# Cross-attention scores on two float32r parts, two heads stacked in 64-row tiles

## What is computed

```
q = heads(x @ Wq)              # 32 heads of 16
k, v = split(ctx @ Wkv)        # heads likewise
q, k = rope(q, pos), rope(k, pos)
p = softmax(q @ k.T / sqrt(16))
out = (p @ v) @ Wout + bout    # then x = layernorm(x + out)
```

## Time and profile before

| | us |
|---|---|
| median of 3 runs | 3319.63 |
| lowest, highest | 3304.61, 3321.81 |
| profiled execution | 3316.54 |
| its span | 3314.8 |
| cross attention in it | about 2415 to 3120 |

### The profile page before, as it was taken

One profiled execution on the slowest core, in us unless ns is written; L12 is line 12 of the kernel. 1 busy time (PEld: TensorE's weight loads), 2 busy tenths in 40 slices (PEclk: granted clock), 3 DMA queues, 4 the chain that ended last, 5 costly groups with the idle time before them and its releaser, 6 DMA issues.

```text
span 3314.8 us, 50665 instructions
## 1 busy us (share of the span) xinstructions
PE 2716.1 (82%) x20138; PEld 1454.0 (44%) x20154; DVE 1958.6 (59%) x3064; ACT 1433.1 (43%) x2577; POOL 1177.7 (36%) x1118
## 2 busy tenths in 40 slices
PE   5788888876677676589988898888768989899787
PEld 3565656553223232268845444444433333333244
DVE  3323232333689889956526566656655657476477
ACT  3232333320545555423426262635315546465555
POOL 0443333441566666600023625243243424241000
PEclk8888888887888888799998999998879989899999
DMA  2222222130330304032332424243155435252301
GB/s 87 71 59 62 52 78 60 47 87 14 121 116 13 127 26 140 13 140 95 137 108 86 128 90 125 93 122 130 39 117 107 105 69 112 61 109 53 118 26 39
DMA packets 209370, 280.04 MB, mean 84 GB/s; under 512 B 84640, under 2 KB 111680, under 8 KB 208240
## 3 DMA queue, kind: packets, MB, share of 16 engines
q1 hardware_dynamic: 209136, 276.81, 29.4%
HBM read 192.08 MB, written 59.12 MB: 76 GB/s over the span
## 4 chain that ended last, share of the span: by engine, by line
PE 39%; DVE 10%; issue 5%; ACT 4%; POOL 2%; DMA 1%; SPq 0%; ACTq 0%; DVEq 0%; POOLq 0%
PE ps L236 7%; PE ps L3368 4%; PE ps L1846 4%; PE ps L1857 4%; PE ps L3355 4%; PE ps L3341 3%; PE ps L3300 3%; PE ps L3332 2%; PE ps L2512 1%; ACT arena L3446 1%; PE ps L2520 1%; DVE arena L2775 1%; DVE arena L1434 1%; DMA arena<-arena 1%; DVE arena L2773 1%
## 5 line engine op out<-in xcount | busy, mean ns | idle before, releaser
L236 PE MATMUL ps<-arena 128*128 128x512 f32 (+3 forms) x1280 | 473.6, 522 | 18.3 <-ACT arena L2612 6.1
L3545 DVE TENSOR_REDUCE arena<-ps 128x1 f32<-128x512 f32 x512 | 330.3, 685 | 229.2 <-PE ps L3341 227.8
L3446 ACT ACTIVATE arena<-ps 128x512 f32<-128x512 f32 x512 | 287.8, 597 | 283.2 <-PE ps L3355 279.7
L1466 POOL TENSOR_TENSOR arena<-arena 128x1024 f32<-128x1024 f32 x128 | 311.0, 2430 | 192.9 <-DVE arena L1458 192.9
L1482 PE MATMUL ps<-arena 128*128 128x512 f32 x512 | 267.2, 662 | 55.8 <-POOL arena L1466 55.5
L1458 DVE TENSOR_TENSOR_SCAN arena<-ps,arena 128x1024 f32<-128x1024 f32 x128 | 291.5, 2278 | 32.9 <-ACT ps L1449 32.9
L236 PEld LDWEIGHTS ps<-arena 128*128 128x128 f32 (+2 forms) x1296 | 193.2, 154 | 252.3 <-issue 172.9
L1449 ACT ACTIVATE ps<-arena 128x511 f32<-128x511 f32 x256 | 165.1, 679 | 188.3 <-DVE arena L1458 188.1
L576 POOL TENSOR_TENSOR arena<-arena 128x31 f32<-128x31 f32 (+15 forms) x217 | 130.1, 600 | 324.2 <-DMA arena<-d_a 307.8
L3355 PE MATMUL ps<-arena 99*128 99x512 bf16 x512 | 198.4, 390 | 45.3 <-ACT arena L3446 33.4
L3341 PE MATMUL ps<-arena 96*128 96x512 bf16 x512 | 201.4, 395 | 19.1 <-issue 15.4
(11 more groups left out here) (352 smaller groups left out, 5254.1 us busy)
## 6 DMA issues: line engine op xcount, KB each, us to landing
arena<-d_bc SPq DMA_DIRECT2D x32, 1024.0 KB, 5.7
arena<-d_x SPq DMA_DIRECT2D x24, 1024.0 KB, 6.8
arena<-d_parts SPq DMA_DIRECT2D x192, 128.0 KB, 4.6
d_x<-arena SPq DMA_DIRECT2D x64, 256.0 KB, 2.5
arena<-arena SPq DMA_DIRECT2D x128, 128.0 KB, 2.1
arena<-in_D_wlm SPq DMA_DIRECT2D x12, 1024.0 KB, 6.6
d_parts<-arena SPq DMA_DIRECT2D x32, 384.0 KB, 2.4
d_signs<-arena SPq DMA_DIRECT2D x32, 256.0 KB, 2.1
```

The lines of the kernel that those rows point to most:

```text
L236: ins = pe.e.matmul(ps[:m, :n], lhsT(k), rhs(k), start=(k == 0), stop=(k == chunks - 1))
L1466: pool.e.tensor_tensor(h, h, s.bc[:, turn % s.SLOTS, 1], ALU.mult).then_inc(*pool.up("scan_hC"))
L3446: act.e.activation(s.E[:, k % 2, j], s.rexp.bank((u, i)), ACT.Exp).then_inc(*s.rexp.empty(act, (u, i)))
L3545: dve.e.tensor_reduce(s.mx[:, u % 2, t, h:h + 1], s.rmax.bank((u, m)), AX.X, ALU.max, negate=True).then_inc(*s.rmax.empty(dve, (u, m)))
```

## The change

The scores are made on two float32r parts in place of three bfloat16 parts: high x high, high x low and low x high, 3 x 16 = 48 rows, and two rows more for the maximum. Even heads lie on partitions 0 to 49, odd heads on partitions 64 to 113, so each score matmul takes one 64-row half of the array (tile size 64 x 128, tile position row 0 or row 64), and the two of a pair write different PSUM banks. The PE program issues two exp scores and then two max scores, and the odd pieces of both steps come after that. The maximum scores of two heads alternate, and so do the reduces. rope() has two operations where it had four behind the rotation. The stacked loads are again six DMAs of 128 KB per unit and side, in runs of 2 KB where they were 1 KB; what is written to DRAM before them is 512 KB in place of 384 KB. The ones come by two DMAs at the start of the stage (sp_one_rows), and the memsets for them go. The stage's buffers become tensors of their own at fixed places (PLACED), and two of them go.

```diff
-    Q_PARTS = (0, 1, 0, 2, 1, 0)
-    K_PARTS = (0, 0, 1, 0, 1, 2)
-    N = 6 * 16
+    Q_PARTS = (0, 0, 1)
+    K_PARTS = (0, 1, 0)
+    N = 3 * 16
...
-        s.Qs, s.Ks = carve(s.SLOTS, s.HU, L, dt=BF16), carve(s.SLOTS, s.HU, L, dt=BF16)
+        s.Qs, s.Ks = carve(s.SLOTS, s.HU // 2, L, dt=F32R), carve(s.SLOTS, s.HU // 2, L, dt=F32R)
...
-        for a in range(3):
-            sp.e.dma_start(s.Qs[96 + a:97 + a, u % s.SLOTS, s.G * half:s.G * (half + 1)],
-                           s.mT[s.G * a:s.G * (a + 1), half, :]).then_inc(*sp.up(f"cross_max_rows{half}", 16))
+        for p in range(2):
+            at = 64 * p + s.N
+            sp.e.dma_start(s.Qs[at:at + 2, u % s.SLOTS, 2 * half:2 * half + 2].bitcast(F32),
+                           s.mT[4 * p:4 * p + 4, half, :].bitcast(F32)).then_inc(*sp.up(f"cross_max_rows{half}", 16))
...
-            sp.e.dma_start(dst[16 * a:16 * a + 16], d[:, :, part, :].rearrange("h d l -> d h l")).then_inc(*sp.up(f"cross_stack_{'qk'[w]}", 16))
+            for p in range(2):
+                at = 64 * p + 16 * a
+                sp.e.dma_start(dst[at:at + 16].bitcast(F32), d[p::2, :, part, :].rearrange("h d l -> d h l")).then_inc(*sp.up(f"cross_stack_{'qk'[w]}", 16))
+
+    def sp_one_rows(self, sp):
+
+        s = self
+        sp.e.wait_ge(*sp.at_all("cross_ones"))
+        for p in range(2):
+            at = 64 * p + s.N
+            sp.e.dma_start(s.Ks[at:at + 2].rearrange("p a h l -> p (a h) l").bitcast(F32), spread(s.one[:2], 1, s.SLOTS * s.HU // 2)).then_inc(*sp.up("cross_one_rows", 16))
...
-        hi, mid, lo = (s.parts[:, w, a] for a in range(3))
+        hi, lo = (s.parts[:, w, a] for a in range(2))
         e.tensor_copy(hi, s.m1[:, w]).then_inc(*eng.up_step("cross"))
         eng.e.wait_ge(*eng.at_step("cross"))
-        e.tensor_tensor(s.rest[:, w], s.m1[:, w], hi, ALU.subtract).then_inc(*eng.up_step("cross"))
-        eng.e.wait_ge(*eng.at_step("cross"))
-        e.tensor_copy(mid, s.rest[:, w]).then_inc(*eng.up_step("cross"))
-        eng.e.wait_ge(*eng.at_step("cross"))
-        e.tensor_tensor(lo, s.rest[:, w], mid, ALU.subtract).then_inc(*eng.up(f"cross_parts_{n}"))
+        e.tensor_tensor(lo, s.m1[:, w], hi.bitcast(F32), ALU.subtract).then_inc(*eng.up(f"cross_parts_{n}"))
...
-        s, slot, h, t = self, u % self.SLOTS, m // T, m % T
+        s, slot = self, u % self.SLOTS
+        hh, t, p = m // (2 * T), m // 2 % T, m % 2
...
-        pe.e.matmul(s.rmax.bank((u, m)), s.Qs[:s.N, slot, h, t * P:(t + 1) * P], s.Ks[:s.N, slot, h, :],
+        rows = slice(64 * p, 64 * p + s.N)
+        pe.e.matmul(s.rmax.bank((u, m)), s.Qs[rows, slot, hh, t * P:(t + 1) * P], s.Ks[rows, slot, hh, :],
...
-        pe.e.matmul(s.rexp.bank((u, i)), s.Ks[:s.N + 3, slot, s.G * g + j, k * P:(k + 1) * P], s.Qs[:s.N + 3, slot, s.G * g + j, :],
+        hh, p = 2 * g + j // 2, j % 2
+        rows = slice(64 * p, 64 * p + s.N + 2)
+        pe.e.matmul(s.rexp.bank((u, i)), s.Ks[rows, slot, hh, k * P:(k + 1) * P], s.Qs[rows, slot, hh, :],
...
-            for m in range(s.STEPS):
+            for m in range(1, s.STEPS, 2):
                 if s.unit(i) is not None:
+                    s.pe_exp(pe, i, m - 1)
                     s.pe_exp(pe, i, m)
                 if s.unit(i + 1) is not None:
+                    s.pe_max(pe, i + 1, m - 1)
                     s.pe_max(pe, i + 1, m)
                 if m % s.G == 1:
...
-                if m in misc:
-                    s.pe_misc(pe, misc[m])
+                for at in (m - 1, m):
+                    if at in misc:
+                        s.pe_misc(pe, misc[at])
...
-        e.tensor_copy(s.identb, s.ident).then_inc(*dve.up("cross_identb"))
-        for a in range(2):
-            e.memset(s.ones[:, a], s.ONES).then_inc(*dve.up("cross_ones"))
         s.rope(dve, 0, 1)
-        for a in range(2, s.SLOTS):
-            e.memset(s.ones[:, a], s.ONES).then_inc(*dve.up("cross_ones"))
...
-                    h, t = m // T, m % T
+                    h, t = m // (2 * T) * 2 + m % 2, m // 2 % T
```

More of the change, by code:

```diff
@@ L3029 @@
     VW = 32
[L3030 to L3031 removed]
+    ONCE = ("cross_weights", "cross_late", "cross_ones", "cross_one_rows", "cross_half_pi")
     EARLY = ("cross_weights", "cross_x", "cross_pos", "cross_ctx")
@@ L3048, in __init__ @@
         s.rows_from = carve.at
-        s.Qs, s.Ks = carve(s.SLOTS, s.HU, L, dt=BF16), carve(s.SLOTS, s.HU, L, dt=BF16)
+        s.Qs, s.Ks = carve(s.SLOTS, s.HU // 2, L, dt=F32R), carve(s.SLOTS, s.HU // 2, L, dt=F32R)
         s.rows_to = carve.at
-        s.ones = carve.t[96:99, carve.at - s.SLOTS * s.HU * L // 2:carve.at].rearrange("p (a n) -> p a n", a=s.SLOTS)
-        s.wo, s.identb, s.half_pi, s.xT = carve(C, D), carve(P, dt=BF16), carve(1), carve(C, L)
+        s.one = carve(L)
+        s.wo, s.half_pi, s.xT = carve(C, D), carve(1), carve(C, L)
         s.cos, s.sin = carve(2, L), carve(2, L)
-        s.raw, s.m1, s.m2, s.rest = carve(2, L), carve(2, L), carve(2, L), carve(2, L)
-        s.parts = carve(2, 3, L, dt=BF16)
-        s.mx, s.mr = carve(2, T, s.HU), carve(T, s.G)
-        s.mp = carve(2, T, 3, s.G, dt=BF16)
-        s.mT = carve(2, L, dt=BF16)
+        s.raw, s.m1, s.m2 = carve(2, L), carve(2, L), carve(2, L)
+        s.parts = carve(2, 2, L, dt=F32R)
+        s.mx = carve(2, T, s.HU)
+        s.mp = carve(2, T, 2, 2, 2, dt=F32R)
+        s.mT = carve(2, L, dt=F32R)
         s.rs = carve(T, s.G)
@@ L3310, in pe_misc @@
             pe.e.wait_ge(*R.at_free(pe, name))
-            if u == half == 0:
-                pe.e.wait_ge(*pe.at_all("cross_identb"))
             for t in range(T):
-                ins = e.transpose(ps.bitcast(BF16)[:3 * s.G, t * P:(t + 1) * P], s.mp[:, half, t].rearrange("p a h -> p (a h)"), s.identb)
+                ins = e.transpose(ps[:2 * s.G, t * P:(t + 1) * P], s.mp[:, half, t].rearrange("q p a h -> q (p a h)").bitcast(F32), s.ident)
         elif what == "turn":
@@ L3351, in pe_exp @@
             pe.e.wait_ge(*pe.at_all("cross_ones"))
+            pe.e.wait_ge(*pe.at_all("cross_one_rows"))
         if k == j == 0:
@@ L3426, in act_misc @@
                 act.e.wait_ge(*act.on(f"cross_max_rows{name[2]}", u - 1))
-            ins = e.activation(s.mT[:3 * s.G, name[2]], ps.bitcast(BF16)[:3 * s.G, :L], ACT.Copy)
+            ins = e.activation(s.mT[:2 * s.G, name[2]], ps[:2 * s.G, :], ACT.Copy)
         else:
@@ L3480, in dve_before @@
         s, e = self, dve.e
+        e.memset(s.one[:2], 1.0).then_inc(*dve.up("cross_ones"))
         e.memset(s.V[:, :, :, :, 16:17], 1.0).then_inc(*dve.up("cross_ones"))
@@ L3524, in dve_parts @@
             dve.e.wait_ge(*s.ring.at_filled(dve, ("mT", u - 1, half)))
-        mx = s.mx[:, u % 2, :, s.G * half:s.G * (half + 1)]
+        mx = s.mx[:, u % 2, :, s.G * half:s.G * (half + 1)].rearrange("q t (h p) -> q t p h", p=2)
         dve.e.wait_ge(*s.rmax.at_emptied(dve, (u, (half + 1) * s.STEPS // 2 - 1)))
-        mp = s.mp[:, half]
-        e.tensor_copy(mp[:, :, 0, :], mx).then_inc(*dve.up_step(st))
+        hi, lo = s.mp[:, half, :, :, 0, :], s.mp[:, half, :, :, 1, :]
+        e.tensor_copy(hi, mx).then_inc(*dve.up_step(st))
         dve.e.wait_ge(*dve.at_step(st))
-        e.tensor_tensor(s.mr, mx, mp[:, :, 0, :], ALU.subtract).then_inc(*dve.up_step(st))
-        dve.e.wait_ge(*dve.at_step(st))
-        e.tensor_copy(mp[:, :, 1, :], s.mr).then_inc(*dve.up_step(st))
-        dve.e.wait_ge(*dve.at_step(st))
-        e.tensor_tensor(mp[:, :, 2, :], s.mr, mp[:, :, 1, :], ALU.subtract).then_inc(*dve.up(f"cross_max_parts{half}"))
+        e.tensor_tensor(lo, mx, hi.bitcast(F32), ALU.subtract).then_inc(*dve.up(f"cross_max_parts{half}"))
     def dve_all(self, dve):
```

11 lines of the change are left out of this document (5 added, 6 removed).

## The result

The changed kernel takes 3347.34 us (median of 4 runs, 3344.05 to 3357.28), the kernel before 3319.64 us (3304.61 to 3321.81). The ratio is 1.0098, with a 95% interval of 1.0062 to 1.0135 (the two medians alone give 1.0083): slower by about 1%. Forecast were 3306 us and a range from 3282 to 3345. The time lies outside the range, and on the other side of no change.

What follows compares the result with a forecast made beforehand. The prediction took a loop of values matmul, exp score, exponentials and freed bank as the bound. Units +5, batch ends −17, front −1 and last unit +1 sum to −12 us; forecast 3306 us, range 3282 to 3345.

Steps and rivals of the forecast that it cites:

- What bounds the kernel: Plain units: a loop of values matmul, exp score, two exponentials and a freed bank, 3.11 us, sets the pace.
- The price of a score: Score matmuls on PE: a pair in 0.22 us, 0.11 each; a first score after another shape pays +0.11.
- rival 1: Score pairs: halves run one after the other, 0.22 apart; about 3355 us, break-even at 0.14 between partners; chance 0.12.
- the tail term: Loop-bound intervals, fourth exp score to values matmul: 0.11 + 0.11 + 0.31 = 0.53 us against 0.54, nothing gained.
- The PE-bound intervals: Plain unit: steps 13 to 17 from 4.63 to 4.43 us (−0.2); steps 5 to 9 and 9 to 13 together −0.15.
- The change of tile shape: PE, between matmuls of different tile shape: costs 0.09 us, 0.31 where 0.22 is usual.
- the dearer case: Change of tile shape drains TensorE: 0.16 us each, five times 0.07 more a unit, about 5 us in all.
- Batch ends: Iterations 4 and 8: new order covers 4.9 of 5.64 us of waits and shortens the long y by 3.1; −8 each.
- The third boundary: Batch end at iteration 12, where the y pieces stand without xT: −1 us.
- Front: Start of the stage: rope's two operations fewer save 2.1 us once, loads stay as they were; net −1.
- The clock: Plain units: clock expected to stay at 1.00; a fall got chance 0.07, argued against from the exp-only stretch.
- rival 2: Plain units: clock falls as work per score shrinks and gaps remain; +42 us, 3348 us; chance 0.07.

Runs made afterwards that it cites:

- the second pair of profiles: The changed kernel and the kernel before, each run once more unchanged; the two profiles differ by 30.6 us.
- the filler: Changed kernel with unread whole-array matmuls added ahead of mT, turn and aT from iteration 13 on; 3371.55 us in one run.
- other banks: Changed kernel with three PSUM banks for exp scores and two for max scores, in place of two and three; 3323.59 us, ratio 1.0033.

## Why the prediction was wrong

**What bounds the kernel: right.** The loop of bank, score, exponential and values matmul sets the plain unit. Two scores now go at once, and the units grew all the same.

**The price of a score: wrong, and the step with the largest share in the units.** I took 0.11 from score to score. The partner costs 0.003, so the lower bound (free) holds and not the 0.11 that I took; the Trainium skill, "TensorE: Matmul & The Clock Gate", section "Part 3: Packing small matmuls — row/col tiling", had 4 ns, and the trace agrees, now with 128 columns. But the next pair comes 0.33 after a pair whose loads were not hidden, not 0.22. That is 0.17 a score, past the 0.14 at which rival 1 broke even. The step that failed is the weight load: I counted the unhidden load once a loop, at its head, where it is (0.10). At the tail I wrote 0.11 + 0.11 + 0.31 = 0.53; it is 0.33 + 0.32 = 0.65, since the last exp score also waits for a bank and its load shows too. Averaging a pair's 0.22 over its two scores hid that. Of the +1.1 a unit that was missing, the tail term is +0.12 in each of the five loop-bound intervals, 0.6.

**The PE-bound intervals: two of three wrong.** Steps 13 to 17 went from 4.63 to 4.86, not to 4.43. I let the two exp scores behind the values matmul go together; but in the trace the second starts 0.56 after the first, when its bank is free, and V starts 2.21 after the values matmul, not 1.81. From there to the end it is 2.65, near the 2.62 that I had. So the interval belongs to the loop as well. Steps 9 to 13 likewise (+0.17), and only steps 5 to 9 gained (−0.21, more than I had). Together +0.19 for −0.35: another 0.5.

**The change of tile shape: right.** It was taken at 0.09, with 0.16 as the dearer case. The changed kernel shows 0.32 from the last max score to the values matmul, as before, and 1.98 from V to the next score where it had 1.78, the 0.20 that I had added for shape and load; the dearer case didn't come.

**Batch ends: right in mechanism, in part by luck in the number.** −7.5 each for −8 in the profiled execution, 26.10 us for 26.3, and the y pieces at 3.70 for 3.6. 3.5 of the 5.64 us of waits were covered, not 4.9: the third y piece has no values matmul ahead of it and waits its 1.38 as before. What made up for it is a term that I had left out: of the 34.30 us, the y pieces (read to the next start) lost 3.3, near the 3.1 that I had, and all the rest lost 1.4. In the second pair of profiles the two ends gained 5.9 and 5.2 only. The third boundary gave −0.5 for −1.

**Front: right, and small.** −0.5 in the first pair of profiles, −2.1 in the second, for −1, and the loads as they were.

**The clock: the largest miss.** I gave a fall in the units 0.07 and argued against it from the exp-only stretch at clock 1.00. In plain units it stayed at 1.00 in the first profile, and fell in one of seven (0.95) in the second. It fell where the projections have ended: iteration 13 (+9.6, of which about 9 by the filler's comparison), the last unit (+4.1) and the stage behind (+7.0), and in both profiles. The term that I had for all this was +1, and "work after the stage is untouched" held for the program but not for its clock. The stretch that I took as evidence was one that the change itself alters: its scores were matmuls on 99 rows of the array, and are now on 50. It is not that two now go at once: with that taken away, the clock is as low. Iteration 0 too is 3.4 longer, at clock 0.78 where it was 0.89; of this 2.4 come with the order alone (45.2 us, 0.85).

**The sum.** On the scale of the profiled execution 3304.5 was expected and 3347.87 measured, 43.4 more: 8.9 in the stages ahead (chance), 0.5 in the front, 12.6 in the units (17.6 measured in iterations 0 to 3, 5 to 7, 9 to 11 and 14 for +5), 1.6 at the batch ends, and 20.7 measured in iteration 13, the last unit and the tail for +1. Rival 1's price was near (3355), yet not by its mechanism; rival 2's was the mechanism in part, at another place.

**What stays open.** Why the clock falls. In iteration 13 it takes tiles and paired order together, and matmuls on the whole array raise it again. In the last unit and behind it, the clock is lower with tiles in either order, but the filler's work did not stop it, and the changed kernel with other banks has 1.00 there and a tail of 198.5. So the tiles alone don't make it.
